# One GNN kernel: the order of work per visit in its edge passes is written anew

## The reference, cut to what matters

```python
def _gatv2(x, src, dst, edge_attr, Wl, bl, Wr, br, We, att, bo):
    xl = x @ Wl.T + bl
    xr = x @ Wr.T + br
    e = edge_attr @ We.T
    m = xl[src] + xr[dst] + e
    score = jnp.where(m > 0, m, NEG_SLOPE * m) @ att
    smax = jax.ops.segment_max(score, dst, num_segments=N)
    smax = jnp.where(jnp.isfinite(smax), smax, 0.0)
    es = jnp.exp(score - smax[dst])
    denom = jax.ops.segment_sum(es, dst, num_segments=N)
    alpha = es / (denom[dst] + 1e-16)
    out = jax.ops.segment_sum(alpha[:, None] * xl[src], dst, num_segments=N)
    return out + bo
h = relu(_gatv2(x, ..., Wl1, ...)); h = _instance_norm(h)
h2 = relu(_gatv2(h, ..., Wl2, ...) + x @ Wskip.T + bskip)
```

## Time and profile before

| what | value |
|---|---|
| median of 3 runs | 7471.15 us (7457.06 to 7473.19) |
| profiled execution, span of the core | 7464.2 us |
| edge passes in it | 177 to 2902 us and 3018 to 5742 us |
| busy, share of the span | PE 79%, PEld 54%, DVE 56%, ACT 36%, POOL 41% |
| DVE, mean of one | L913 363 ns, L914 365, L919 417, L925 153, L927 282, L933 747 and its read 83, L879 281, L880 393 |
| ACT, mean of one | L973 722 ns, L975 279, L982 383, L987 597, L993 492 |
| POOL, mean of one gather | 957 ns, 3,168 of them |

### The profile page before, as it was taken

One profiled execution on the slowest core, in us unless ns is written; L12 is line 12 of the kernel. 1 busy time (PEld: TensorE's weight loads), 2 busy tenths in 40 slices (PEclk: granted clock), 3 DMA queues, 4 the chain that ended last, 5 costly groups with the idle time before them and its releaser, 6 DMA issues. The chain is left out here.

```text
span 7464.2 us, 173944 instructions
## 1 busy us (share of the span) xinstructions
PE 5871.2 (79%) x40704; PEld 4054.3 (54%) x40705; DVE 4175.9 (56%) x13350; ACT 2649.9 (36%) x5416; POOL 3043.6 (41%) x3185
## 2 busy tenths in 40 slices
PE   2877778777777875677777787778788679999699
PEld 1555555555555554455555555555556663333689
DVE  6555555555555556455555555555555347888432
ACT  1333333333333332333333333333333118888210
POOL 2455555555555552555555555555553000000000
PEclk8889999999999887889998988998989889999899
DMA  3233333333333322333333333333332733332579
GB/s 82 71 80 75 80 82 82 75 82 80 74 81 83 82 73 54 75 83 79 75 81 80 75 82 82 82 76 80 82 73 59 281 141 110 115 121 94 205 287 361
DMA packets 701430, 768.13 MB, mean 103 GB/s; under 512 B 372274, under 2 KB 623257, under 8 KB 676256
## 3 DMA queue, kind: packets, MB, share of 16 engines
q1 hardware_dynamic: 553907, 574.53, 25.2%
q0 software_dynamic: 101376, 104.01, 7.3%
q10 hardware_dynamic: 46062, 88.56, 3.3%
HBM read 674.60 MB, written 88.81 MB: 102 GB/s over the span
## 5 line engine op out<-in xcount | busy, mean ns | idle before, releaser
L823 POOL DMA_INDIRECT gat_rows<-rows_scr,gat_idx x3168 | 3031.0, 957 | 2686.3 <-issue 916.2
L1049 PE MATMUL gat_counts<-adj_hot_key,adj_hot_lo 128*128 128x392 bf16 x2416 | 808.8, 359 | 930.1 <-DVE adj_hot_key L880 443.0
L973 ACT ACTIVATE gat_weights<-gat_masked,gat_newtop 128x512 f32<-128x512 f32 x792 | 571.5, 722 | 1466.4 <-DVE gat_newtop L933 1167.2
L1049 PEld LDWEIGHTS gat_counts<-adj_hot_key,adj_hot_lo 128*128 128x128 bf16 x2416 | 241.3, 100 | 1560.5 <-issue 1309.0
L987 ACT ACTIVATE gat_weightsT<-gat_tps 128x512 f32<-128x512 f32 x792 | 472.7, 597 | 1478.8 <-issue 655.8
L1094 PE MATMUL gat_sps<-gat_relu,gat_att 128*128 128x256 f32 x3168 | 970.0, 431 | 6.0 <-issue 2.7
L925 DVE COPY gat_oldtop<-gat_top 128x1 f32 x792 | 121.1, 153 | 1512.8 <-issue 860.5
L880 DVE TENSOR_SCALAR adj_hot_key<-adj_iota_key,adj_winbase,adj_key 128x392 bf16<-128x392 int16 x2416 | 950.0, 393 | 3.5 <-issue 3.3
L1114 PE MATMUL gat_aps<-gat_rows,gat_weightsT 128*128 128x65 f32 x6288 | 883.2, 288 | 16.2 <-issue 15.8
L1114 PEld LDWEIGHTS gat_aps<-gat_rows,gat_weightsT 128*128 128x128 f32 x6288 | 863.9, 213 | 9.6 <-issue 9.4
L879 DVE TENSOR_SCALAR adj_hot_lo<-adj_iota_lo,adj_low 128x128 bf16<-128x128 int16 x2416 | 677.8, 281 | 285.8 <-issue 232.3
(11 more groups left out here) (355 smaller groups left out, 7143.5 us busy)
## 6 DMA issues: line engine op xcount, KB each, us to landing
gcn_sum_adj<-adj_scr SPq DMA_DIRECT2D x98, 1568.0 KB, 8.5
gat_dstb<-dst_scr SPq DMA_DIRECT2D x792, 128.0 KB
gat_ea<-in_ea SPq DMA_DIRECT2D x792, 128.0 KB
gin_sum_adj<-adj_scr SPq DMA_DIRECT2D x49, 1568.0 KB, 8.5
adj_scr<-adj_tiles ACTq DMA_DIRECT2D x48, 1568.0 KB
at_adj<-adj_scr SPq DMA_DIRECT2D x84, 896.0 KB
gat_rows<-rows_scr,gat_idx POOLq DMA_INDIRECT x3168
gat_xr<-xr_scr SPq DMA_DIRECT2D x1584, 24.0 KB
```

The lines of the kernel that those rows point to most:

```text
L823: pool.indirect_dma_start(rows[:, u, c, 0:ROW], None, rows_d, bass.IndirectOffsetOnAxis(ap=idx[:, u, c:c + 1], axis=0)).then_inc(s_g[u], 16)
L973: act.activation(wts[:, j, :], masked[:, j, :], ACT.Exp, bias=newtop[:, j:j + 1], scale=-1.0)
L1049: return pe.matmul(bank[:, 0:WD * NT], plan.hot_lo[:, slot, :], plan.hot_key[:, slot, :], start=start, stop=False)
```

## The change

The order of work in a visit is written anew for PE, DVE and ACT; SP and POOL are not edited. What each engine does in visit n now:

- PE: message n, window n, turn n-1, score n, sum n-1.
- DVE: top of n-2, relu n-1, masks n, old top n-1, accumulator n-3, min/max n-1, one-hots n.
- ACT: slope n, eviction of turn n-1, eviction of window n, shrink and exponential n (the drain behind them goes; the exponential, now last, raises `weight`).

The table of delays, the waits, the buffers' indices, the initial values of semaphores and buffers and the carried registers follow from that (`DRAIN` 3). At the end of a pass DVE raises `top` and `acc` once more and ACT `relu`, so that the waits of the last visit can be met.

```diff
-DRAIN = 4
+DRAIN = 3
...
-    delay = {"masked": 0, "message": 0, "fifth": 0, "relu": 1, "score": 1, "top": 2, "weight": 2, "turned": 2, "evac": 2,
-             "sum": 3, "acc": 4, "topped": 3, "olded": 2}
+    delay = {"masked": 0, "message": 0, "fifth": 0, "relu": 1, "score": 0, "top": 1, "weight": 0, "turned": 1, "evac": 1,
+             "sum": 1, "acc": 3, "topped": 2, "olded": 1}
...
-                    dve.wait_ge(s["top"], count("top", step, 3))
+                    dve.wait_ge(s["top"], count("top", step, 2))
+                    dve.nop(nofuse=True)
+                    dve.tensor_copy(top[:, bass.ds(tb, 1)], newtop[:, (u - 2) % 2:(u - 2) % 2 + 1]).then_inc(s["topped"], 1)
+
+                    dve.wait_ge(s["fifth"], count("fifth", step, 1))
+                    j, o = (u - 1) % 2, (u - 1) % 4
+                    dve.tensor_tensor(relu[:, j, :], mps[j][:, 0:GE // 2], relu[:, j, :], ALU.max).then_inc(s["relu"], 1)
+
                     dve.wait_ge(s_loaded, step + 1)
-                    dve.nop(nofuse=True)
-                    dve.tensor_copy(top[:, bass.ds(tb, 1)], newtop[:, (u - 3) % 2:(u - 3) % 2 + 1]).then_inc(s["topped"], 1)
                     dve.tensor_scalar(hit[:, u % 4, :], near, node, None, ALU.is_equal)
...
-                    dve.wait_ge(s["fifth"], count("fifth", step, 1))
-                    j = (u - 1) % 2
-                    dve.tensor_tensor(relu[:, j, :], mps[j][:, 0:GE // 2], relu[:, j, :], ALU.max).then_inc(s["relu"], 1)
-
-                    dve.wait_ge(s["topped"], count("topped", step, 3))
-                    dve.wait_ge(s["sum"], count("sum", step, 4))
+                    if woven:
+                        window_chunks(dve, span, step + w_first)
...
+                    dve.wait_ge(s["topped"], count("topped", step, 2))
                     dve.nop(nofuse=True)
-                    j, o = (u - 2) % 2, (u - 2) % 4
                     dve.tensor_copy(oldtop[:, o:o + 1], top[:, bass.ds(tm, 1)]).then_inc(s["olded"], 1)
+                    dve.wait_ge(s["sum"], count("sum", step, 3))
...
-                    dve.wait_ge(s["olded"], count("olded", step, 2))
-                    dve.wait_ge(s["score"], count("score", step, 2))
+                    dve.wait_ge(s["olded"], count("olded", step, 1))
+                    dve.wait_ge(s["score"], count("score", step, 1))
...
+            def slope(step, u):
                 j = u % 2
                 act.wait_ge(s["message"], count("message", step, 0))
                 act.wait_ge(s["score"], count("score", step, 2))
                 act.activation(relu[:, j, :], mps[j][:, 0:GE // 2], ACT.Copy, scale=0.2).then_inc(s["fifth"], 1)
 
-                j = (u - 2) % 2
+                j = (u - 1) % 2
+                act.wait_ge(s["turned"], count("turned", step, 1))
+                act.wait_ge(s["sum"], count("sum", step, 3))
+                act.activation(wtsT[:, j, :], tps[:], ACT.Copy).then_inc(s["evac"], 1)
+
+            def weigh(step, u):
+                j, o = u % 2, u % 4
+                act.wait_ge(s["top"], count("top", step, 0))
+                act.wait_ge(s["acc"], count("acc", step, 4))
+                act.activation(shrink[:, o:o + 1], oldtop[:, o:o + 1], ACT.Exp, bias=newtop[:, j:j + 1], scale=-1.0)
                 act.wait_ge(s["turned"], count("turned", step, 2))
-                act.wait_ge(s["sum"], count("sum", step, 4))
-                act.activation(wtsT[:, j, :], tps[:], ACT.Copy).then_inc(s["evac"], 1)
+                act.activation(wts[:, j, :], masked[:, j, :], ACT.Exp, bias=newtop[:, j:j + 1], scale=-1.0
+                               ).then_inc(s["weight"], 1)
...
+                    if woven:
+                        count_edges(step, counts[u % 2])
+
                     j = (u - 1) % 2
-                    pe.wait_ge(s["relu"], count("relu", step, 1))
-                    pe.wait_ge(s["top"], count("top", step, 3))
+                    pe.wait_ge(s["weight"], count("weight", step, 1))
+                    pe.wait_ge(s["evac"], count("evac", step, 2))
+                    for c in range(GC):
+                        last = pe.transpose(tps[:, c * P:(c + 1) * P], wts[:, j, c * P:(c + 1) * P], ident[:])
+                    last.then_inc(s["turned"], 1)
+
+                    j = u % 2
+                    pe.wait_ge(s["relu"], count("relu", step, 0))
+                    pe.wait_ge(s["top"], count("top", step, 2))
                     for h in range(2):
                         last = pe.matmul(sps[j][:, h * (GE // 2):(h + 1) * (GE // 2)], att[:, h, :], relu[:, j, :],
                                          start=True, stop=True)
                     last.then_inc(s["score"], 1)
...
-                    pe.wait_ge(s["evac"], count("evac", step, 3))
-                    pe.wait_ge(s["acc"], count("acc", step, 4))
+                    pe.wait_ge(s["evac"], count("evac", step, 1))
+                    pe.wait_ge(s["acc"], count("acc", step, 2))
```

More of the change, by code:

```diff
@@ L843, in _ @@
             dve.drain().then_inc(s_ones, 1)
-            dve.sem_inc(s["sum"], FREE + 3)
+            dve.sem_inc(s["sum"], FREE + 1)
             dve.sem_inc(s["message"], FREE)
@@ L852, in _ @@
             dve.memset(relu[:, 1, :], 0.0)
[L853 removed]
+            dve.memset(wts[:, 1, :], 0.0)
             dve.memset(newtop[:], CEIL)
@@ L857, in _ @@
             dve.memset(mps[1][:, 0:GE // 2], 0.0)
-            dve.memset(sps[0][:], 0.0)
+            dve.memset(sps[1][:], 0.0)
             dve.wait_ge(s_w, 32)
@@ L938, in turn @@
                         dve.reg_load(pair, words[0:1, bass.ds(i * (TURN // 2) + u // 2 + 1, 1)])
+                    dve.wait_ge(s["topped"], count("topped", step, 2))
+                    dve.nop(nofuse=True)
+                    dve.tensor_copy(oldtop[:, o:o + 1], top[:, bass.ds(tm, 1)]).then_inc(s["olded"], 1)
+                    dve.wait_ge(s["sum"], count("sum", step, 3))
+                    a = acc[:, bass.ds(ta, 1), :].rearrange("p a f -> p (a f)")
+                    dve.scalar_tensor_tensor(a, a, shrink[:, (u - 3) % 4:(u - 3) % 4 + 1],
+                                             aps[:, 0:D + 1], ALU.mult, ALU.add).then_inc(s["acc"], 1)
+                    dve.wait_ge(s["olded"], count("olded", step, 1))
+                    dve.wait_ge(s["score"], count("score", step, 1))
+                    dve.nop(nofuse=True)
+                    dve.tensor_tensor_reduce(masked[:, j, :], sps[j][:], miss[:, o, :], 1.0, oldtop[:, o:o + 1],
+                                             ALU.add, ALU.min, accum_out=newtop[:, j:j + 1]).then_inc(s["top"], 1)
                     if woven:
@@ L948, in _ @@
                 turn(i + TAIL // TURN, False)
+            dve.drain()
+            for n in ("top", "acc"):
+                dve.sem_inc(s[n], 1)
         @block.scalar
@@ L967, in _ @@
             act.sem_inc(s_stored, 16)
-            def visit(step, u):
-                j = (u - 2) % 2
[L971 to L977, removed]
+            def slope(step, u):
                 j = u % 2
@@ L1006, in half_tile @@
                 for u in range(RING):
-                    visit(first_step + u, u)
+                    slope(first_step + u, u)
                     empty(first_step + u, u, slot, a + u)
+                    weigh(first_step + u, u)
                 with nc.allow_non_contiguous_dma(reason="half a tile, once"):
@@ L1019, in _ @@
                     step = i * (2 * RING) + (u + RING * second)
-                    visit(step, u)
+                    slope(step, u)
                     empty(step, u, slot, u)
+                    weigh(step, u)
                 store(step, (i + second) * 16 + 16,
@@ L1028, in _ @@
                 for u in range(TURN):
-                    visit(i * TURN + (TAIL + u), u)
+                    slope(i * TURN + (TAIL + u), u)
+                    weigh(i * TURN + (TAIL + u), u)
+            act.drain().then_inc(s["relu"], 1)
             act.wait_ge(s_stored, (half + 1) * 16 + 16)
@@ L1096, in visits @@
                     last.then_inc(s["score"], 1)
[L1097 to L1101, removed]
-                    pe.wait_ge(s["evac"], count("evac", step, 3))
-                    for c in range(GC):
-                        last = pe.transpose(tps[:, c * P:(c + 1) * P], wts[:, j, c * P:(c + 1) * P], ident[:])
-                    last.then_inc(s["turned"], 1)
-                    j = (u - 3) % 2
-                    v = slice((u - 3) % RING, (u - 3) % RING + 1) if back is None or u >= 3 else bass.ds(back + u, 1)
-                    if first and u < 3:
+                    j = (u - 1) % 2
+                    v = slice((u - 1) % RING, (u - 1) % RING + 1) if back is None or u >= 1 else bass.ds(back + u, 1)
+                    if first and u < 1:
                         continue
-                    pe.wait_ge(s["evac"], count("evac", step, 3))
-                    pe.wait_ge(s["acc"], count("acc", step, 4))
+                    pe.wait_ge(s["evac"], count("evac", step, 1))
```

(7 more changed lines are left out.)

12 lines of the change are left out of this document (1 added, 11 removed).

## The result

The changed kernel took 8,190.79 us (8,176.43 to 8,223.77) beside 7,472.17 us for the kernel before: ratio 1.0974, 95% interval 1.0947 to 1.1002, slower. The forecast was 7,423 and faster, so the direction was wrong. In the profiled run, whose span is 8,174.6 us, the first pass makes 1,284 / 4 = 321 visits in the 2,500 us that held 362: 7.79 us a visit for 6.90.

The account below looks back on a forecast made before the run. It took POOL's loop of gather burst and late `sum` as the bound: 6.69 + 0.07 + 0.02 + 0.06 = 6.84 us a visit for 6.90, times 792, -48 us, so 7,423 us; 8-in-10 range 7,200 to 8,200.

Parts of the forecast that it names:

- The bound: POOL's loop in the edge passes: gather burst 4.69 us, `sum` seen 1.4 later, restart 0.6, together 6.69 us a visit.
- the first line of the layout: Start of the laid-out visit, t = 0: `message`(n), `sum`(n-2), `turned`(n-1) seen together; slope, relu until 0.9 us, eviction until 1.05.
- rival 3: Edge visits: only `turned` slips, eviction and sums 1.6 us after the release in one of three; +420, about 7,890; chance 0.10.
- mostly is not: Claim that `turned` mostly isn't seen late: transposes ended at 1596.61, 3.1 us into a burst, their eviction started at 1596.64.
- Rival 2: Edge visits: sums slip behind the release, 9.7 us a visit, priced at a third; +740, about 8,210; chance 0.19.
- Price (a): `sum` seen inside a burst makes POOL run two without pause: 6.81 us in a fifth of visits, +0.02 a visit.
- What goes at L925 on DVE comes back: DVE's idle time at L925 moves behind relu(n), ahead of masks, accumulate and min/max; only score(n) waits for relu itself.
- Rival 1: Lateness isn't tied to POOL, pace falls to the engines: 5.0 us a visit, 5,966; milder form 6,758; chance 0.15.

Follow-up runs that it names:

- p_sum: Kernel before with only the sums and accumulator moved one visit nearer, sums right behind their turn; 8,894.22 us beside 7,400.39.
- f_delay: Changed kernel with sums two visits on (n-2 instead of n-1), still behind score n; 7,544.84 us beside 7,406.48 for the kernel before.
- p_score: Kernel before with only the score moved, score n behind turn n-2 in its message's own visit; 8,161.57 us beside 7,400.39.
- after3: The changed kernel run again unchanged, on the second kind of chip; 6,092.57 us beside 5,999.07 for the kernel before.
- after: The changed kernel itself, on the first kind of chip; 8,190.79 us beside 7,472.17 for the kernel before.
- w3_before: Kernel before with three memsets with drains on POOL behind each burst of gathers, second kind of chip; 8,692.04 us beside 5,999.6.
- w2_before: Kernel before with two memsets with drains on POOL behind each burst of gathers, second kind of chip; 8,313.1 us beside 5,999.6.
- mem_after: Changed kernel with each gather replaced by three memsets and drains on POOL, first kind of chip; 6,457.55 us beside 7,406.48.

## Why the prediction was wrong, step by step

- The bound was read rightly for the first kind: 5,964 with one gather, and 402 of 790 visits keep 6.83 us against 6.69 foreseen.
- The step that failed is the first line of the layout, "`message`(n), `sum`(n-2), `turned`(n-1) are seen" all at the release, with sums n-1 following inside the burst. It holds only if the sums end before the release. In 220 of the 256 late visits they wait for the eviction, which starts when `turned` is seen, 1.1 us after the burst (median), and takes 0.6; then come their own 1.1 to 2.0 us, and POOL starts 0.8 later. With sums right behind their turn in the old order, 90% of the visits are so (`p_sum`); one visit between them, and 18 are left (`f_delay`).
- I had the mechanism as rival 3 at 0.10, with 1.6 us in one visit of three. Its frequency was right (256 of 790), its size is 2.04. I gave it the least chance of the three because `turned` "mostly is not" late. That is so, but the old trace held the rest: by a count from its timeline, the eviction starts after the burst and over 1 us behind its transposes in about 210 of its 790 visits. It cost nothing there, since the sums were a visit behind. The prediction went by two visits, and the earlier trace rows, and not by a count.
- Rival 2 has the right total, 8,210, and the range's upper end of 8,200 takes in the 8,191, partly by luck: rival 2 has the sums wait behind a late message in a third of the visits. On the new order the score ahead of the sums loses only 1.9% (`f_delay`). Its mechanism shows in the 58 long stalls and, on the old order, in `p_score`.
- Price (a), bursts without a pause: estimated at 6.81 us a visit from the passes' starts, 16 us in all. Measured 5.51 for the burst itself and 12.50 for the one behind it, 231 us in all. The pairs at the starts did not show the late message behind them.
- "What goes at L925 on DVE comes back" was called harmless. The accumulate behind the relu made PE's sums wait for it (299 us in `after3`), on a kind where the whole loss is 93 us.
- PE's clock was not in the sum: granted 0.84 for 0.91 in the window. The sums take about 1.97 us in half of the late visits and 1.1 in the others; against the usual 1.10 that is an estimated 110 of the 522 us, by the means 1.52 and 1.10. The clock fell where the waits grew; no run separates the two.
- Rival 1's 5,966 is close to what chips of the second kind show for the kernel before, 6,000; nothing in the trace of one chip could tell that. The Trainium skill's tail of some tens of ns on a matmul's increment (TensorE: Matmul & The Clock Gate, "The cost: per-tile semaphore tail") agrees with the 0.03 us there and with memsets; with gathers on the first kind the 3.8 us of the late visit above contradict it.

## What to carry to other kernels

A semaphore that arrives late was harmless here while a whole visit lay between it and its first reader: pipeline depth pays for lateness, and an order that shortens delays spends it. Count how often an increment is late over all visits, not in one, and ask where in the burst the new order will put it. Measure on more than one chip before a bound is called the kernel's: the same kernel took 7,400 us on some chips and 6,000 on two others.

## What the runs showed of the hardware

- While POOL issues indirect transfers, PE's increments were late on some chips (a `turned` of 1512.96 met at 1516.73) and not on others (1552.51 met at 1552.54, amid gathers without pause). What differs between the chips stays open. The stages behind the edge passes take the same time on both kinds (1,727 us behind the last sums in `after`, 1,743 in `after3`).
- Memsets of about the same length on POOL don't do it. Without SP's transfers the changed kernel lost less, 1.059 for 1.097; whether they make increments later was not shown.
- Behind gathers, a memset with a drain on POOL was followed by 1.46 us of nothing (median of `w3_before`; 1.47 in `w2_before`, up to 4.80 and over in single visits). Without gathers, in `mem_after`, the next group of memsets began 0.15 us on.
